# Key and query biases of seven layers folded into the projection weights of a linear attention stack

## The reference, cut to what matters

```python
for i in range(8):
    residual = x
    Q  = elu(x @ Wq[i] + bq[i]) + 1
    Kf = elu(x @ Wk[i] + bk[i]) + 1
    V  = x @ Wv[i] + bv[i]
    KV, sumK = sum(Kf * V, axis=1), sum(Kf, axis=1)
    att = Q * KV / (Q * sumK + 1e-6)
    x = layer_norm(gelu(att @ Wo[i] + bo[i]) + residual, ln1_s[i], ln1_b[i])
    residual = x
    h = gelu(gelu(x @ W1[i] + b1[i]) @ W2[i] + b2[i])
    x = layer_norm(h + residual, ln2_s[i], ln2_b[i])
```

## Time and profile before

| | |
|---|---|
| median of 3 runs | 3271.7 us (3268.28 to 3273.61) |
| the profiled execution | 3271.77 us, its span 3269.6 us |
| mean granted TensorE clock | 0.961 of full speed |
| layer phase, from the first to the last x_hi | 825.6 to 3061.1 us |
| busy shares of the whole span | PE 90%, PEld 60%, DVE 82%, ACT 74%, POOL 26% |

### The profile page before, as it was taken

How to read it: one execution, slowest core, us unless ns; L and a number is a source line. 1 busy time by engine, 2 the same in 40 slices (tenths; PEclk the granted TensorE clock), 3 DMA queues, 4 the chain that set the end, 5 groups by cost and what they waited for, 6 DMA issues and landing times. The chain is left out here.

```text
span 3269.6 us, 50808 instructions
## 1 busy us (share of the span) xinstructions
PE 2953.8 (90%) x14297; PEld 1961.7 (60%) x14297; DVE 2672.6 (82%) x10489; ACT 2419.0 (74%) x4498; POOL 853.8 (26%) x1032
## 2 busy tenths in 40 slices
PE   6999998364799999999999999999999999999868
PEld 5777776253466666665666666566666666655545
DVE  4656565864689999998999999899999899989967
ACT  5888886122588888887888888788888878877743
POOL 2444443266111111112111111211111121122326
PEclk9999999587899999999999999999999999999988
DMA  1000000323100000000000000000000000000001
GB/s 56 1 0 0 0 0 1 111 36 64 46 1 1 22 12 1 20 7 8 1 26 8 1 20 7 8 1 27 7 1 20 7 7 1 20 7 7 1 1 39
DMA packets 32201, 49.49 MB, mean 15 GB/s; under 512 B 5395, under 2 KB 21859, under 8 KB 31718
## 3 DMA queue, kind: packets, MB, share of 16 engines
q1 hardware_dynamic: 26342, 42.64, 3.9%
q0 software_dynamic: 5632, 4.20, 1.0%
HBM read 38.31 MB, written 8.51 MB: 14 GB/s over the span
## 5 line engine op out<-in xcount | busy, mean ns | idle before, releaser
L2070 DVE TENSOR_SCALAR t_feat_q<-t_recip,t_neg_mean 128x256 f32<-128x256 f32 x1024 | 410.0, 462 | 111.9 <-ACT t_recip L1887 109.2
L1624 PE MATMUL t_o_ps<-t_feat_q,t_wo 128*128 128x512 f32 x1008 | 469.1, 598 | 7.7 <-issue 4.1
L1879 ACT ACTIVATE t_recip<-t_feat_q,t_z_scale 128x256 f32<-128x256 f32 x1024 | 434.8, 499 | 4.4 <-DVE t_feat_q L2070 3.7
L1865 ACT ACTIVATE t_exp_k<-t_k_ps 128x1024 f32<-128x1024 f32 x256 | 259.7, 1015 | 230.4 <-PE t_k_ps L1598 230.4
L2033 DVE CUSTOM_DVE_ANT_0 t_junk<-t_v_ps,t_feat_k 128x256 f32<-128x256 f32 x1024 | 390.1, 418 | 12.3 <-PE t_v_ps L1598 12.0
L2290 POOL TENSOR_TENSOR t_var_eps<-t_moments,t_ln_eps 128x4 f32<-128x4 f32 x128 | 67.5, 527 | 1224.1 <-DVE t_moments L2081 1224.1
L2023 DVE SCALAR_TENSOR_TENSOR t_feat_k<-t_exp_k,t_k_ps 128x256 f32<-128x256 f32 x1024 | 368.9, 416 | 15.7 <-ACT t_exp_k L1865 15.7
L1869 ACT ACTIVATE t_exp_q<-t_q_ps 128x1024 f32<-128x1024 f32 x256 | 261.5, 1022 | 86.5 <-PE t_q_ps L1598 85.5
L2059 DVE SCALAR_TENSOR_TENSOR t_feat_q<-t_exp_q,t_q_ps 128x1024 f32<-128x1024 f32 x256 | 312.7, 1221 | 8.8
L1624 PEld LDWEIGHTS t_o_ps<-t_feat_q,t_wo 128*128 128x128 f32 x1008 | 191.9, 191 | 178.8 <-issue 158.4
L243 POOL TENSOR_TENSOR a_probs<-a_probs,a_inv 128x256 f32<-128x256 f32 (+1 forms) x256 | 209.2, 839 | 275.6 <-DVE a_inv L340 275.6
(11 more groups left out here) (441 smaller groups left out, 7223.6 us busy)
## 6 DMA issues: line engine op xcount, KB each, us to landing
t_raw_w<-in_wk SPq DMA_DIRECT2D x8, 512.0 KB, 3.7
t_raw_w<-in_wq SPq DMA_DIRECT2D x8, 512.0 KB, 4.6
t_raw_w<-in_wv SPq DMA_DIRECT2D x8, 512.0 KB, 5.5
t_raw_o<-in_wo SPq DMA_DIRECT2D x8, 512.0 KB, 3.7
t_raw<-in_w SPq DMA_DIRECT2D x16, 256.0 KB, 2.7
x<-in_x SPq DMA_DIRECT2D x4, 512.0 KB, 7.0
tokens_dram<-r_hn SPq DMA_DIRECT2D x8, 256.0 KB, 2.3
e_w_raw<-in_fc_w SPq DMA_DIRECT2D x4, 512.0 KB, 3.9
```

Of the source, the lines that this page charges most:

```text
L1624: last = pe.matmul(out[:], wo[:, chunk, :], feat_q[:, s, chunk, :], start=(chunk == 0), stop=(chunk == NC - 1), skip_group_check=True)
L1865: act.activation(exp_k[:], k_ps[:], ACT.Exp, bias=-1.0).then_inc(c["k_exp"], 1)
L1879: last = act.activation(recip[:, q % 2, k * UNIT + n * SEQ:k * UNIT + (n + 1) * SEQ], feat_q[:, s, chunk, cols], ACT.Ln, bias=1.0, scale=z ...
L2070: last = dve.tensor_scalar(feat_q[:, s, chunk, cols], recip[:, q % 2, k * UNIT + n * SEQ:k * UNIT + (n + 1) * SEQ], -1.0, neg_mean[:, s, n ...
```

## The change

The state that stage A reads is no longer x but z + 1, where z is the second layer norm before its scale s and shift c; so x = s*z + c. Then x W + b + 1 = (z + 1) W' holds with one corrected matrix W'. The ones column of z + 1 is not an extra row: since z of a token has the mean 0 over its 128 channels, the sum over the channels of z + 1 is 128, and a row vector divided by 128 and added to every row of W' comes out as a bias. W' = fold_m applied to the raw weights (a diagonal of s, plus (c - s)/128 everywhere) plus the bias rows divided by 128.

- Layer 0 keeps `biases`, the other seven drop them, and `keys` and `queries` wait for their own bank alone.
- In steps 1 to 6 of each of the layers 0 to 6, `fold_piece` makes one sixth of the next layer's W' on TensorE in the bank `o_ps`: keys, queries, values, each in two halves of 512 columns. It has one float32 matmul, and for keys and queries a bfloat16 matmul ahead of it that adds the bias (`bias_pick` has 1/128 in three rows). ScalarE copies the piece out as the high part, VectorE subtracts for the low part, and `project(0)` waits for that, since it needs the bank.
- `make_fold` writes fold_m once per layer on ScalarE (step 0). `restore_x` turns z + 1 in `state_t` into x in place on ScalarE, once per step from layer 1 on, before stage C adds the residual. The write of the state loses its scale and shift and adds 1.
- The loop turns at multiples of 8 steps: 8 unrolled, three turns of 16, 8 unrolled.
- At the entry GpSimd makes `bias_pick` and `fold`. In the expert phase `AHEAD` becomes 4, `gate_rows(0)` and `split_rows(1)` stand before `mark(4)`, and `split_biases` behind `gate_rows(2)`.

```diff
-        AHEAD = 3
+        AHEAD = 4
...
+            pool.memset(g["t_bias_pick"][:], 0.0).then_inc(c["pick_zeroed"], 1)
+            pool.wait_ge(c["pick_zeroed"], 1)
+            for k in range(4):
+                pool.memset(g["t_bias_pick"][32 * k:32 * k + 3, k, :], 1.0 / D).then_inc(c["pick_made"], 1)
...
         def run(eng, step):
 
-            for t in range(4):
+            for t in range(PER):
                 step(t, t)
             with eng.Fori(0, LAYERS // 2 - 1) as two:
-                for i in range(4, 4 + 2 * PER):
+                for i in range(PER, 3 * PER):
                     step(two * (2 * PER) + i, i)
...
+        def folds(at):
+
+            return 1 <= at % PER <= 6 and at < UNITS - PER
...
-                sp.wait_ge(c["w_ready"], thrice)
+                sp.wait_ge(c["w_ready"], sp.snap(6 * n + 1))
...
+            def keys(t, s, w, q, biased):
+                if not biased:
+                    pe.wait_ge(c["k_ready"], 4 * t + q + 1)
                 for half in range(2):
-                    last = three_pass(k_ps[:, half * UNIT:(half + 1) * UNIT], 0, 2 * q + half, s, w, False)
+                    last = three_pass(k_ps[:, half * UNIT:(half + 1) * UNIT], 0, 2 * q + half, s, w, not biased)
                 last.then_inc(c["k_filled"], 1)
...
+            def fold_piece(t, at):
+
+                kind, half = piece_of(at)
+                layer = layer_of(t) + 1
+                pe.wait_ge(c["raw_w_in"], 48 * layer + 49)
+                pe.wait_ge(c["fold_ready"], layer + 1)
+                if at >= 2:
+                    pe.wait_ge(c["y1_ready"], t - 2 + 2)
+                if kind < 2:
+                    pe.wait_ge(c["raw_b_in"], 64 * layer + 65)
+                    pe.matmul(o_ps[:], bias_pick[:, 2 * kind + half, :], raw_b[:].rearrange("p q c -> p (q c)"), start=True, stop=False,
+                              skip_group_check=True)
+                pe.matmul(o_ps[:].rearrange("p (q c) -> p q c", c=P), fold_m[:], halves(raw_w[:, kind, :])[:, :, half, :],
+                          start=(kind == 2), stop=True, skip_group_check=True).then_inc(c["w_folded"], 1)
...
                 if A:
-                    biases(t, w, 1)
-                    pe.wait_ge(c["w_ready"], 3 * layer_of(t) + 4)
+                    if biased:
+                        biases(t, 1)
+                    pe.wait_ge(c["w_ready"], 6 * layer_of(t) + 7)
                     values(t, s, w, 0, 0)
-                    keys(t, s, w, 1)
-                    queries(t, s, w, 1)
+                    if folds(at):
+                        fold_piece(t, at)
+                    keys(t, s, w, 1, biased)
+                    queries(t, s, w, 1, biased)
...
+                if folds(at):
+                    pe.wait_ge(c["w_ready"], 6 * layer_of(t) + 6 + at % PER + 1)
                 if B:
                     project(t - 1, r, 0)
...
+            def restore_x(t):
+
+                layer = layer_in_range(t - PER)
+                place = g["state_t"][:, bass.ds(place_of(t), 1), :]
+                act.wait_ge(c["x_split"], t + 2)
+                act.activation(place, place, ACT.Identity, bias=fold[:, bass.ds(layer, 1), 0], scale=params[:, bass.ds(layer, 1), 8])\
+                   .then_inc(c["restored"], 1)
...
                 if B:
                     exp_z(t - 1, 0)
+                if folds(at):
+                    split_piece(t, at)
                 if A:
                     exp_keys(t, 1)
...
                     exp_keys(t, 3)
-                    for k in range(3):
-                        if prepares(at, k):
-                            split_weights(layer_of(t) + 1, 1 - half_of(at), k)
                     exp_queries(t, 3)
+                    if at >= PER:
+                        restore_x(t)
+                    if at % PER == 0 and at < UNITS - PER:
+                        make_fold(t)
                 if B:
                     log_z(t - 1, r, 3)
...
                 if B:
                     attention(t - 1, r, 0)
+                if folds(at):
+                    split_piece(t, at)
                 if A:
                     feature_k(t, s, 1)
...
                 if C:
+                    dve.wait_ge(c["restored"], t - 2 + 2)
                     dve.wait_ge(c["y1_ready"], t - 2 + 2)
```

More of the change, by code:

```diff
@@ L1483, in stack_phase @@
         free_seen = sem("t_free_seen")
-        raw_w, raw_b, w_hi, w_lo, b3, ones_b, ln_eps, carrier, pool_carrier, params, bv_all = (
-            g["t_" + n] for n in "raw_w raw_b w_hi w_lo b3 ones_b ln_eps carrier pool_carrier params bv_all".split())
+        raw_w, raw_b, w_hi, w_lo, b3, ones_b, ln_eps, carrier, pool_carrier, params, bv_all, bias_pick, fold, fold_m = (
+            g["t_" + n] for n in ("raw_w raw_b w_hi w_lo b3 ones_b ln_eps carrier pool_carrier params bv_all "
+                                  "bias_pick fold fold_m").split())
         block = ctx.enter_context(nc.Block())
@@ L1503, in half_of, with piece_of, halves @@
             return at // PER % 2
-        def prepares(at, kind):
-            return at % PER == 4 + kind and at < UNITS - PER
-        def prepares_bias(at):
-            return at % PER == 3 and at < UNITS - PER
+        def folds(at):
+            return 1 <= at % PER <= 6 and at < UNITS - PER
+        def piece_of(at):
+            return (at % PER - 1) // 2, (at % PER - 1) % 2
+        def halves(row):
+            return row.rearrange("p (q h c) -> p q h c", h=2, c=P)
         def active(at, lag):
@@ L1590, in biases @@
                         rows = slice(32 * (2 * kind + half), 32 * (2 * kind + half) + 3)
-                        pe.matmul(out[:, half * UNIT:(half + 1) * UNIT], b3[rows, half_of_w, q, :], ones_b[rows, :],
+                        pe.matmul(out[:, half * UNIT:(half + 1) * UNIT], b3[rows, 0, q, :], ones_b[rows, :],
                                   start=True, stop=False, skip_group_check=True)
@@ L1702, in step @@
                     values(t, s, w, 1, 0)
[L1703 to L1704 removed]
+                    if biased:
+                        biases(t, 2)
+                    queries(t, s, w, 2, biased)
                 if C:
@@ L1710, in step @@
                 if A:
-                    keys(t, s, w, 2)
+                    keys(t, s, w, 2, biased)
                 if E:
@@ L1727, in step @@
                     values(t, s, w, 2, 0)
-                    biases(t, w, 3)
-                    keys(t, s, w, 3)
-                    queries(t, s, w, 3)
+                    if biased:
+                        biases(t, 3)
+                    keys(t, s, w, 3, biased)
+                    queries(t, s, w, 3, biased)
                     values(t, s, w, 2, 1)
@@ L1856, in modulate, with split_piece, make_fold @@
                 act.activation(g["f_h_hi"][n], g["state_t"][:, n, :], ACT.Copy).then_inc(f["h_hi_ready"], 1)
-            def split_weights(layer, w, k):
-                act.wait_ge(c["raw_w_in"], 48 * layer + 49)
-                act.activation(w_hi[:, w, k, :], raw_w[:, k, :], ACT.Copy).then_inc(c["w_hi_ready"], 1)
+            def split_piece(t, at):
+                kind, half = piece_of(at)
+                act.wait_ge(c["w_folded"], 6 * layer_of(t) + at % PER + 1)
+                act.activation(halves(w_hi[:, 1 - half_of(at), kind, :])[:, :, half, :], o_ps[:].rearrange("p (q c) -> p q c", c=P), ACT.Copy)\
+                   .then_inc(c["w_hi_ready"], 1)
+            def make_fold(t):
+                layer = layer_in_range(t)
+                act.wait_ge(c["w_ready"], 6 * layer_of(t) + 7)
+                act.activation(fold_m[:], g["ident"][:], ACT.Identity, bias=fold[:, bass.ds(layer, 1), 1], scale=params[:, bass.ds(layer, 1), 8])\
+                   .then_inc(c["fold_ready"], 1)
+            def restore_x(t):
[4 more added lines that the diff above has]
+                   .then_inc(c["restored"], 1)
             def exp_keys(t, q):
@@ L1936, in step @@
                     act.activation(g["state_t"][:, bass.ds(place_of(t - 4), 1), :], m0[:].unsqueeze(1), ACT.Identity,
-                                   bias=param(t - 4, 9), scale=param(t - 4, 8)).then_inc(c["state_t_ready"], 1)
+                                   bias=1.0).then_inc(c["state_t_ready"], 1)
                 if leaves(at - 1):
@@ L2005, in _, with split_piece @@
         def _(dve):
-            def copy_bias(layer, w):
-                dve.wait_ge(c["raw_b_in"], 64 * layer + 65)
-                dve.tensor_copy(b3[:, w, :, :], raw_b[:]).then_inc(c["b3_ready"], 1)
-            def split_weights(layer, w, k):
-                dve.wait_ge(c["w_hi_ready"], 3 * layer + k + 2)
-                dve.tensor_tensor(w_lo[:, w, k, :], raw_w[:, k, :], w_hi[:, w, k, :].bitcast(F32), ALU.subtract).then_inc(c["w_ready"], 1)
+            def split_piece(t, at):
+                kind, half = piece_of(at)
+                out, hi = (halves(w[:, 1 - half_of(at), kind, :])[:, :, half, :] for w in (w_lo, w_hi))
```

(2 more changed lines are left out.)

62 lines of the change are left out of this document (33 added, 29 removed), and 1 row of the table names.

## The result

The changed kernel took 3247.2 us in the median of four runs (3246.6 to 3248.7), the kernel before 3271.2 on the same chip: a ratio of 0.9927, with an interval of 0.9914 to 0.9939. It is 24 us faster. The forecast was 5.5 us slower; the time lies inside the whole range (3240 to 3308) and outside the sum's own (3262 to 3295), on the other side of no change.

What follows compares the result with a forecast made beforehand. VectorE and ScalarE together were taken to close the layer step. Terms -28.6 - 1.1 + 45.5 - 9.2 + 1.5 - 2.6 gave +5.5 us, 3277.3 us; the sum's own range was 3262 to 3295, the whole range 3240 to 3308.

Steps and rivals of the forecast that it cites:

- expert phase: Four gathers ahead take one gather out of POOL's row between additions: -2.6 us (0 to -5.1).
- step gain of 0.55 us: Layer steps without bias groups: 0.37 us ahead of the first queries plus 0.18 at the last keys, in 52 steps -28.6.
- The second stretch: VectorE's own, from layer norm statistics to the end of chunk 3's `feature_q`, with one late wait for keys, 0.18 us.
- The flip of order: Rival: VectorE's `attention(1)` goes ahead of POOL's x_lo if 0.25 us sooner, saving 0.85 per step, 3230 us; chance 0.07.
- the two closed stretches: Layer step: from chunk 3's `feature_q` through TensorE and ScalarE to the statistics, then VectorE's own to the next `feature_q`.
- the price of a piece with its split: Fold matmul on TensorE behind `values(0, 0)`: 0.93 us, plus 0.23 for the bias pick in 28 of 42 steps; 45.5 in all.
- `restore_x` at 0: ScalarE pass ahead of `scale_n1`, near 0.62 us, covered almost exactly by waits there: cost 0, up to 0.62 per step uncovered.
- `make_fold` at 0.2 us each: Seven smaller ScalarE passes at the place of `restore_x`, with no cover left: 0.2 us each, +1.5 (0 to 4.3).
- `project(0)` without a wait for the split: ScalarE's and VectorE's split of the piece ends before TensorE reaches `project(0)`, five us behind: no cost.
- the wait for the last keys gone: VectorE's late wait of 0.18 us for TensorE's last keys disappears, as chunk 3's bias group goes.
- TensorE's order: Rival: TensorE sets the step, so all bias groups count, 96.3 us less; total 3218, step 33.5 or less; chance 0.22.
- ScalarE's stretch: Rival: `restore_x` ahead of `scale_n1` delays chunk 3's `attention`; no step below 35 us, total 3295 or 3307; chance 0.15.

Runs made afterwards that it cites:

- `hole`: The changed kernel with `restore_x` and `make_fold` moved into ScalarE's idle time ahead of the keys of chunk 3; 3243.9 us.
- `early_x_hi`: The changed kernel with ScalarE's x_hi moved ahead of the logarithms of chunk 2; 3232.7 us.
- `early_hole`: The changed kernel with x_hi ahead of the logarithms of chunk 2, and `restore_x` and `make_fold` ahead of the keys of chunk 3; 3221.0 us.

## Why the prediction was wrong, and where it was right

**The step that failed is the step gain of 0.55 us.** It counts the bias matmuls alone, and puts at nothing, without a reason, what else the change takes out of a step. Measured alone, the bias matmuls give 0.63, so that term was nearly right, in part by luck: 0.32 and 0.31 in the two stretches, where the forecast had 0.37 and 0.18. Two things that were not in the sum go with it:

- The write of the state (0.33 to 0.39 us per step). The prediction went through what the change adds on ScalarE and left out that an instruction that stays loses two operands. Its row of 0.78 us is not among the rows read, so the way from it over x_hi and x_lo to `attention` of chunk 1 was not followed. The second stretch was called VectorE's own "with a single late wait"; the 0.85 us by which `attention` of chunk 1 was longer than others is a wait inside a busy row. The Trainium skill ("ScalarE: Activation LUTs", What ACT_TABLE_LOAD costs) says that each operand of one value per partition adds about 93 ns to such an instruction. The rows agree: 0.78 - 0.60 = 0.18 for two.
- TensorE's waits (0.17 us per step). A met wait was taken as free.

In 52 steps the difference of 0.63 us is 33 us; the forecast of +5.5 becomes -27, against -24 measured. Of what is left between, the expert phase did not give its 2.6 us. And the step that swaps the other weights, which the prediction called untouched, gained less than its neighbours: before it took 36.31 to 36.38 us, 1.2 above a plain step, and now 36.58, 1.49 above the step with a piece beside it. There GpSimd goes on behind x_lo with those weights, and `attention` of chunk 1 takes 3.13 us (at 1479.83). The rest is not followed up: the first steps of the phase vary by some us from kernel to kernel (the second one takes 30.8 us in the kernel before, 35.2 in the changed one and 32.6 in `hole`).

**The flip of order** was the rival that came nearest. It had the right pair of rows and the right price of waiting (though VectorE ends 0.95 us behind GpSimd's end in those rows, not 1.06), and named the wrong party: it asked whether VectorE could come sooner and ruled that out, since both hang on the same layer norm. It was GpSimd that came sooner, and by a part of the way: 0.34 of the 0.85. The rule that it drew on, the Trainium skill's ("SBUF — State Buffer", SBUF: two separate sides) that the two engines hold a pair of ports one at a time, is borne out here: `attention` ends 0.94 to 0.95 us behind x_lo in three kernels, and takes 1.14 where x_lo is over (`early_x_hi`). The Trainium skill says it there of certain VectorE instructions only (in a mode that uses two ports, or with two inputs in SBUF); no run here was made to tell these kinds apart.

**Right:** the two closed stretches and their order; the price of a piece with its split (1.11 us for keys and queries, 0.89 for values; forecast 1.16 and 0.93), though half of it would stay without the matmuls; `restore_x` at 0, but by a narrow margin: its row is 0.80 us and not near 0.62 (unlike x_hi it reads a scale and a bias per partition, and 0.80 - 0.62 is again 0.18), and its slot of 1380.64 - 1379.94 = 0.70 us stands against the 0.72 from which it would cost; `make_fold` at 0.2 us each; `project(0)` without a wait for the split; the wait for the last keys gone. **TensorE's order** as the bound falls: the waits ahead of its first queries (0.54) remain, and the plain step is at 33.98, not 33.5 or less. **ScalarE's stretch** did not close in the changed kernel; it did close, by 0.15 us, once VectorE had won 0.5 us, at the place that the rival named (`early_x_hi` against `early_hole`). The expert phase gave 0 in place of -2.6. Some signs that were to show the forecast right came although it was wrong: VectorE is busy 31.35 of 33.98 us in the plain step, 92%, and TensorE 96% where it was 98%. They do not tell 0.55 from 1.18; the plain step's length does.

## What to carry to other kernels

List what a change takes from instructions that stay: an operand, a scale, a wait, a place in the order of waits. Follow the end of each such instruction to whoever waits for it, on engines that look idle too, and read a row that is longer than others of its kind as a wait that the trace doesn't show as one. Where two stretches are nearly closed, a gain on one engine shows up only until the next engine's slack is used up, so the moves have to be made together.

## What the runs showed of the hardware that was not expected

- Two operands read per partition cost a ScalarE instruction on 128x512 elements 0.18 us (0.78 against 0.60), and it started another 0.15 us later behind the TensorE rows that it waited for (0.18 against 0.03). In both kernels with these operands they are taken at an index that changes with the layer; no run tells the operands from the index.
- Two met waits of TensorE that stand behind the one that ends last cost 0.12 us together (0.17 against 0.05 from `feature_q` to the queries).
- A VectorE row can be 0.5 to 0.85 us longer for a GpSimd instruction that started 0.25 to 0.57 us ahead of it, and shows no idle time. Not every row is: in `early_x_hi` x_lo (1371.82 to 1373.10) runs beside `values` and `feature_k`, which take 0.41 to 0.42 us as elsewhere.
